# Layer 0 with its side chains at other steps; the state-space stage with taps stacked in three tiles of 96 rows and another order of projections, sums and skips

## The reference, cut to what matters

```python
xz = x @ in_proj_w.T
xi, z = jnp.split(xz_, 2, axis=-1)
xi = silu(causal_dwconv1d(xi))          # 4 taps
x_dbl = xi @ x_proj_w.T                 # dt, B, C
dt = softplus(x_dbl[..., :1] @ dt_proj_w.T + dt_proj_b)
h[t] = exp(dt * A) * h[t-1] + dt * B * u
y = (h * C).sum(-1) + u * D ; y = y * silu(z)
out = (y_forward + y_backward) @ out_proj_w.T
```

## Time and profile before

| | |
|---|---|
| median of 3 runs | 28376.06 us (28369.96 to 28379.99) |
| the profiled execution | 28380.97 us, its span 28379.2 us |
| PE busy | 21447.4 us (76%) |
| DVE busy | 15597.7 us (55%) |
| ACT busy | 14062.1 us (50%) |
| POOL busy | 9313.7 us (33%) |
| granted TensorE clock, mean | 0.907 of full speed |

### The profile page before, as it was taken

How to read it: one execution, slowest core, us unless ns; L and a number is a source line. 1 busy time by engine, 2 the same in 40 slices (tenths; PEclk the granted TensorE clock), 3 DMA queues, 4 the chain that set the end, 5 groups by cost and what they waited for, 6 DMA issues and landing times. The chain is left out here.

```text
span 28379.2 us, 395153 instructions
## 1 busy us (share of the span) xinstructions
PE 21447.4 (76%) x133726; PEld 8244.4 (29%) x134574; DVE 15597.7 (55%) x17851; ACT 14062.1 (50%) x24598; POOL 9313.7 (33%) x7704
## 2 busy tenths in 40 slices
PE   5777777777544777777775999899934888888899
PEld 2222222222211222222221444444401333333344
DVE  7777777777714777777774555555523333333201
ACT  5667666667533555555553666666622222222111
POOL 4666666666403666666664000100000000000000
PEclk9888888888777999999998999999967999999999
DMA  1000000000192000000002010111086010101101
GB/s 56 9 9 9 9 9 9 9 9 9 54 161 73 6 6 6 6 6 6 6 6 69 22 24 22 24 28 24 21 187 157 23 27 20 29 20 28 38 30 47
DMA packets 862945, 933.77 MB, mean 33 GB/s; under 512 B 279812, under 2 KB 754344, under 8 KB 825984
## 3 DMA queue, kind: packets, MB, share of 16 engines
q1 hardware_dynamic: 824904, 819.95, 13.0%
q0 software_dynamic: 17664, 67.11, 0.8%
q10 hardware_dynamic: 19368, 33.14, 0.4%
HBM read 708.43 MB, written 211.63 MB: 32 GB/s over the span
## 5 line engine op out<-in xcount | busy, mean ns | idle before, releaser
L270 DVE TENSOR_TENSOR l_mx<-l_p_v,l_puN 128x2048 f32<-128x2048 f32 x2560 | 5687.2, 2283 | 1797.8 <-PE l_p_s L485 1464.6
L485 PE MATMUL l_p_s<-l_mx,l_w2z 128*32 128x512 f32 x32768 | 4246.7, 657 | 455.5 <-ACT l_mx L397 282.7
L290 POOL TENSOR_TENSOR l_mx<-l_pv,l_puP 128x2048 f32<-128x2048 f32 x1024 | 3706.4, 3640 | 31.9 <-ACT l_puN L363 16.5
L1650 ACT ACTIVATE l1d_ab<-l1d_pt 128x512 f32<-128x512 f32 x4608 | 2739.5, 599 | 1570.7 <-PE l1d_pt L1488 1484.3
L1583 DVE TENSOR_SCALAR l1d_hat<-l1d_ab 128x512 f32<-128x512 f32 x4608 | 2039.0, 443 | 2092.0 <-ACT l1d_ab L1650 1988.0
L1197 POOL TENSOR_TENSOR l1m_hc<-l1m_hs,l1m_cs 128x512 f32<-128x512 f32 x2304 | 2921.8, 1268 | 9.2 <-DVE l1m_hs L1149 9.1
L1884 PE MATMUL l3a_p<-l3a_xn,l3a_w 128*128 128x512 f32 (+1 forms) x6144 | 2678.8, 599 | 274.6 <-ACT l3a_xn L1775 274.6
L1149 DVE TENSOR_TENSOR_SCAN l1m_hs<-l1m_da,l1m_carry,l1m_pu 128x512 f32<-128x512 f32 x2304 | 2824.1, 1267 | 106.1 <-ACT l1m_da L1063 2.2
L397 ACT ACTIVATE l_mx<-l_mx 128x2048 f32<-128x2048 f32 x1024 | 1945.3, 1906 | 1367.8 <-POOL l_mx L290 1367.0
L1990 POOL DMA_DIRECT2D l3b_xt<-x_after x64 | 33.9, 530 | 7646.2 <-DVE l3b_most L2119 5820.6
L416 ACT ACTIVATE l_mx<-l_pv,l_puP 128x128 f32<-128x128 f32 x8192 | 2443.8, 391 | 0.0
(11 more groups left out here) (304 smaller groups left out, 25533.3 us busy)
## 6 DMA issues: line engine op xcount, KB each, us to landing
n_xt<-x_after SPq DMA_DIRECT2D x48, 2048.0 KB
l3a_xb<-x_after SPq DMA_DIRECT2D x352, 256.0 KB, 4.1
l1o_img<-x_after SPq DMA_DIRECT2D x32, 2032.0 KB, 17.5
l_img<-x_after SPq DMA_DIRECT2D x32, 2032.0 KB, 17.5
n_xt<-in_x_dram SPq DMA_DIRECT2D x16, 2048.0 KB
l_xs<-in_x_dram SPq DMA_DIRECT2D x128, 256.0 KB, 3.0
x_after<-l_ot SPq DMA_DIRECT2D x128, 256.0 KB, 2.4
l1o_img<-x_after SPq DMA_DIRECT2D x16, 2048.0 KB, 16.6
```

Of the source, the lines that this page charges most:

```text
L270: v.tensor_tensor(mx[:, r % QB, :, :, :], columns.unsqueeze(1).broadcast_to([P, 4, G, P]), rows.broadcast_to([P, 4, G, P]), ALU.max).then_ ...
L290: g.tensor_tensor(mx[:, r % QB, :, :, :], pv[:, u, :, :].unsqueeze(1).broadcast_to([P, 4, G, P]), rows.broadcast_to([P, 4, G, P]), ALU.add ...
L485: ins = pe.matmul(p_s[R * q:R * (q + 1), 512 * u:512 * (u + 1)], w2z[:, 31 - r:63 - r], mx[:, r % QB, q, :, :].rearrange("p t v -> p (t v) ...
L1650: act.activation(ab[:, n % 3, :], pt[:, 512 * (n % 3):512 * (n % 3 + 1)], ACT.Abs).then_inc(abs_done, 1)
```

## The change

Layer 0: the string of makers is rotated (the same 20 "v", 8 "g" and 4 "a"), and 14 side steps get other step numbers. State-space: the four taps become rows of three tiles of 96 rows (4 x 72 = 288 = 3 x 96), so `sq` holds four shifted copies of a chunk and is filled by six transfers instead of one; x_proj has three matmuls instead of four; z_proj reads the third tile with zero weights for the rows that it does not need. Four memsets that padded the tiles go, with their waits. z_proj of half 0 moves from p = 0 to p = 1, dt_proj of half 0 from p = 4 to p = 3, the sums over pairs 0 to 3 to p = 5, the sum over pairs 5 and 6 to p = 7, the output projection to p = 8; ScalarE follows; the skip and the gates move by one pair or one part, and dt of half 1 moves on GpSimd from p = 6 to p = 7.

```diff
-MAKERS = "vvgvvavgvvgvvavgvvgvvavgvvgvvavg"
+MAKERS = "agvvvgvvagvvvgvvagvvvgvvagvvvgvv"
...
 (gpsimd)
-                    if before is not None and r == 6:
+                    if before is not None and r == 13:
                         weigh_sums(i - 1)
-                    if before is not None and r == 15:
+                    if before is not None and r == 14:
                         finish(i - 1, 1 - u, before)
-                    if r == 19:
+                    if r == 31:
                         modulate(i, u)
...
 (scalar)
-            prepare = {16: normalise, 21: copy_hT, 28: copy_projections, 31: copy_corrections}
+            prepare = {17: normalise, 19: copy_hT, 26: copy_projections, 28: copy_corrections}
...
-                    if before is not None and r == 6:
+                    if before is not None and r == 5:
                         sigmoids(i - 1, 1 - u)
-                    if before is not None and r == 10:
+                    if before is not None and r == 13:
                         copy_aT(i - 1)
-                    if before is not None and r == 14:
+                    if before is not None and r == 16:
                         copy_z(i - 1)
-                    if r == 18:
+                    if r == 22:
                         copy_mT(i)
...
 (tensor)
-                    if before is not None and r == 3:
+                    if before is not None and r == 7:
                         weighted_sums(i - 1, 1 - u)
-                    if before is not None and r == 6:
+                    if before is not None and r == 8:
                         mix(i - 1, 1 - u)
-                    if r == 9:
+                    if r == 16:
                         modulation(i, u)
-                    if following is not None and r == 13:
+                    if following is not None and r == 16:
                         transposes(i + 1, 1 - u)
-                    if following is not None and r == 20:
+                    if following is not None and r == 22:
                         projections(i + 1, 1 - u)
-                    if following is not None and r == 26:
+                    if following is not None and r == 24:
                         pe.wait_ge(mT_ready, i + 1)
                         corrections(i + 1, 1 - u)
...
+TILE_ROWS = 96
+TAP_PARTS = ((0, 0, 0, 72), (0, 72, 0, 24), (1, 0, 24, 48), (1, 48, 0, 48), (2, 0, 48, 24), (2, 24, 0, 72))
...
-                sp.dma_start(sq[0:R, u, :], seq[at(i)].rearrange("i p n -> (i p) n")).then_inc(s_in[u], 16)
+                taps = (0, 1, 1, 2, 2, 3)
+                rows = seq[at(i)].rearrange("i p n -> (i p) n")
+                for tap, (tile, to, first, n) in zip(taps, TAP_PARTS):
+                    sp.dma_start(sq[to:to + n, u, tile, :], rows[first:first + n, tap:tap + LC]).then_inc(s_in[u], 16)
...
-                for tap in range(4):
-                    ins = pe.matmul(pp[:, :], wtap[:, tap, hf, :], sq[:, un, tap:tap + LC], start=tap == 0, stop=tap == 3)
+                for tile in range(3):
+                    ins = pe.matmul(pp[:, :], wtap[:, tile, hf, :], sq[:, un, tile, :], start=tile == 0, stop=tile == 2)
...
 (tensor, chunk)
                     if p == 0 and not last:
                         x_proj(n, un, 0)
-                        z_proj(n, un, 0)
                     if p == 1:
                         reduce_previous(i, u)
+                    if p == 1 and not last:
+                        z_proj(n, un, 0)
                     if p == 2 and not last:
                         x_proj(n, un, 1)
                         z_proj(n, un, 1)
-                    if p == 3:
+                    if p == 5:
                         reduce(i, u, (0, 1))
+                        reduce(i, u, (2, 3))
+                        reduce(i, u, (4,))
+                    if p == 7:
+                        reduce(i, u, (5, 6))
                     if not last:
+                        if p == 3:
+                            dt_proj(n, un, 0)
                         if p == 4:
-                            dt_proj(n, un, 0)
                             dt_proj(n, un, 1)
...
-                    if p == 5:
-                        reduce(i, u, (2, 3))
-                    if p == 6:
-                        reduce(i, u, (4,))
-                    if p == 7:
+                    if p == 8:
                         out_proj(i, use_of(N, 0) if last else use_of(n, OUT))
-                    if p == 8:
-                        reduce(i, u, (5, 6))
...
 (vector)
-                    if p == 1:
+                    if p == 2:
                         skip(i - 1, 1 - u, 1, i * D_IN + (8 + 4))
```

More of the change, by code:

```diff
@@ L748, in state_space @@
         m = Memory(nc, ctx, "l1m")
-        win = m.sb("win", [P, 4, P])
-        crow = m.sb("crow", [R, 4, 2, P])
-        wtap = m.sb("wtap", [P, 4, 2, P])
+        wx = m.sb("wx", [TILE_ROWS, 3, 2, P])
+        wz = m.sb("wz", [TILE_ROWS, 2, P])
+        crow = m.sb("crow", [TILE_ROWS, 3, 2, P])
+        wtap = m.sb("wtap", [TILE_ROWS, 3, 2, P])
         wdt = m.sb("wdt", [P, 2, 2, P])
@@ L760, in state_space @@
         slt = m.sb("slt", [P, RUNS, 32])
-        sq = m.sb("sq", [P, 2, HALO + LC])
+        sq = m.sb("sq", [TILE_ROWS, 2, 3, LC])
         al = m.sb("al", [NB, 2, D_IN + 1])
@@ L790, in state_space @@
         stored = [m.sem("stored0"), m.sem("stored1")]
-        TILES = 4
-        WEIGHTS = 12
+        LOADS = 16 * len(TAP_PARTS)
+        WEIGHTS = 13
         block = ctx.enter_context(nc.Block())
@@ L861, in z_proj @@
                 into_pp(n, (Z0, Z1)[hf])
-                pe.matmul(pp[:, :], win[:, 2 + hf, :], sq[:, un, HALO:], start=True, stop=True).then_inc(pp_full, 1)
+                pe.matmul(pp[:, :], wz[:, hf, :], sq[:, un, 2, :], start=True, stop=True).then_inc(pp_full, 1)
             def both_halves(out, w, n_in):
@@ L949, in _ @@
             reduce_previous(0, 0, (5, 6))
-            pe.wait_ge(s_in[0], 16)
+            pe.wait_ge(s_in[0], LOADS)
             x_proj(0, 0, 0)
@@ L973, in chunk @@
                     if p == 0 and not last:
-                        pe.wait_ge(s_in[un], jn * 16 + 16)
+                        pe.wait_ge(s_in[un], jn * LOADS + LOADS)
                         x_proj(n, un, 0)
-                        z_proj(n, un, 0)
                     if p == 1:
@@ L1087, in chunk @@
                         decays(n, un, p + 2 - PAIRS)
[L1088 to L1097, removed]
-                    if not last:
+                    if not last:
+                        if p == 0:
+                            gate_x(n, un, 0, True)
+                        if p == 1:
+                            gate_z(n, un, 0, True)
+                        if p == 2:
+                            a_of(n, un, jn)
+                            gate_x(n, un, 1, True)
+                            gate_z(n, un, 1, True)
+                        if p == 3:
+                            softplus_parts(n, 0, True)
                         if p == 4:
-                            softplus_parts(n, 0, True)
                             softplus_parts(n, 1, True)
@@ L1106, in chunk @@
                             c_copy(n, un, True)
+                    if p == 8:
+                        out_copy(j, u, use_of(N, 0) if last else use_of(n, OUT))
             over_chunks(act, chunk)
@@ L1112, in _ @@
         def _(dve):
-            for tile in (win, wtap, sq, wo):
-                dve.memset(tile[:], 0.0).then_inc(padded, 1)
             dve.memset(hc[:], 0.0).then_inc(hc_done, 6)
@@ L1124, in _ @@
             dve.wait_ge(w_load, 16 * WEIGHTS)
-            dve.wait_ge(padded, TILES)
-            for tap in range(4):
-                dve.tensor_tensor(wtap[0:R, tap], win[0:R, 0:2, :], crow[:, tap], ALU.mult)
+            dve.tensor_tensor(wtap[:], wx[:], crow[:], ALU.mult)
             for hi in range(2):
@@ L1203, in chunk @@
                         outputs(i, j, u, p, part, last)
-                        if (p, part) == (1, 0):
+                        if (p, part) == (2, 0):
                             gated(i - 1, 1 - u, 1)
-                        if (p, part) == (8, 0):
+                        if (p, part) == (8, 1):
                             g.wait_ge(pp_drained, (use_of(N, 0) if last else use_of(i + 1, OUT)) + 1)
                             gated(i, u, 0)
-                        if not last and part == 1 and p in (5, 6):
-                            steps(i + 1, 1 - u, p - 5)
+                        if not last and part == 1 and p in (5, 7):
+                            steps(i + 1, 1 - u, p // 7)
             over_chunks(g, chunk)
@@ L2182, in program @@
     sequences(nc, offsets, tables[2], a["gn_offset_w"], a["gn_offset_b"], seq, B)
[L2183 removed]
+    state_space(nc, seq, a["w_x"], a["w_z"], a["conv_rows"], a["conv_b"], a["w_dt"], a["dt_rows"], a["dt_b"], a["w_b"], a["w_c"],
                 a["a_log"], a["keeps"], a["d_skip"], a["w_out"], a["sel"], a["sel_t"], mixed, B)
```

(21 more changed lines are left out.)

15 lines of the change are left out of this document (5 added, 10 removed).

## The result

The changed kernel takes 26044.35 us (median of four runs, 25924.9 to 26065.4) against 28375.78 us: a ratio of 0.917, 95% interval 0.9157 to 0.9184, so 8.3% faster. The forecast was 25755 us with a range of 25350 to 26950; the gain is 2331 us where 2621 were forecast. The profiled execution took 26026.6 us, its span 26024.8 us. The shortest of the four, 25924.9 us, had a mean granted clock of 0.913 where the other three had 0.906 or 0.907.

What follows compares the result with a forecast made beforehand. Waits between in-order queues, not a full engine, were taken to bound both stages. From the profiled 28381 us, 1638 for layer 0 and 985 for the state-space stage came off; median 5 us lower: 25755 us, range 25350 to 26950.

Steps and rivals of the forecast that it cites:

- What bounds the stages: Both stages: no engine is full, so waits between queues that run in order bound them and new places of steps matter.
- Layer 0: First stage: a group falls from 58.4 to 45.5 us because its long waits go; gain 1638 us.
- The walk: One round followed step by step with trace durations; in layer 0 ScalarE's loop came to 44.1 us, VectorE's to 44.2.
- the 2.4 at `mix`: Layer 0 before the change: a further VectorE idle stretch of about 2.4 us, called the rest of the 14.0 a group.
- The state-space stage: Second stage: a chunk falls from 48.66 to 40.9 us; gain 985 us.
- p = 2 to 4: State-space stage: intervals between `replicate` starts, together 14.4 us a chunk for 16.4, with the longest, 7.9, at p = 2.
- I keep that: 40.9: State-space stage: clean chunk of 40.0 us, plus the old mean's excess of 0.95 at granted clock 0.97, gives 40.9.
- The tap tiles: State-space stage: six x_proj records instead of eight, 1.7 us of work less a chunk, places mattering more.
- rows of 72: x_proj in the state-space stage: half the rows of an array do not change a column rate that such rows already have.
- The rule against it: TensorE's clock: short pauses between matmul groups can make it swing; the forecast held that by the rows it rises.
- Rival 2: TensorE gets a clock of about 0.8 in both stages, some 50 us a group and 44 a chunk: 26720; chance 0.12.
- Hidden costs: State-space stage: six transfers hidden, else 460 us at most; two more table loads already in the walk; GpSimd's wait covered.

Runs made afterwards that it cites:

- sums_back: The changed kernel with `weighted_sums` and `mix` back behind steps 3 and 6 of layer 0 on TensorE; 26420.61 us, 0.9313 of the kernel before.
- makers_only: The kernel before with the new string of makers in layer 0, side steps at their old numbers; 27421.35 us, ratio 0.9671.
- sides_only: The kernel before with the new numbers of layer 0's side steps, old string of makers; 27747.81 us, ratio 0.9783.
- z_twice: The changed kernel with the z projection of half 0 computed twice into the same bank; 25769.09 us, 0.9085 of the kernel before.
- order_only: The kernel before with the new order of the state-space stage on all engines, four taps and one load as before; 27391.03 us, ratio 0.9659.
- x_four: The changed kernel with the first matmul of each x_proj done twice, three tiles and six loads kept; 25917.59 us, 0.9136 of the kernel before.

## Why the prediction was right, and where its sum was off

- **What bounds the stages**: right. Waits between queues were the reserve, 14 us a group and 15 us a chunk over the floors; the change took 13.4 and 5.1 us of them.
- **Layer 0**: right step by step. The walk closed at 44.2 us; I added 1.3 for table loads and hand-overs, and 0.8 was needed (45.02). Each wait that the walk named came as walked: none at `weighted_sums`, 1.2 us at `mix` (1.4), 2.26 at `normalise` (2.2), none at the change of group. `sums_back` shows the first of these to be cause and not company, and `makers_only` with `sides_only` give 12.2 of the 13.4 us one by one. One sum of the reading before does not close: 4.6, 5.6, 2.9 and 2.4 us are 15.5, not 14.0, so the 2.4 at `mix` is not "the rest". The group that was read is longer (59.9 us from one first VectorE step to the next) than the mean. Two slips of rounding do not matter: 58.4 less 44.2 is 14.2, not 14.1, and 28381 less 1638, 985 and 5 is 25753, not 25755.
- **The state-space stage**: direction right, size off by 336 us (649 for 985). The intervals of the walk against the trace are p = 0: 3.6 and 3.85; p = 1: 5.1 and 4.87; p = 2 to 4: 14.4 and 18.7 (10.09 + 5.31 + 3.34); p = 5: 7.4 and 7.41; p = 6 to 8: 9.5 and 9.39. So one term was wrong, p = 2 to 4, and within it the step "I keep that: 40.9", which carried the old clock of 0.97 into an order that had new pauses. TensorE loses its full clock in each chunk, mostly there; `z_twice` shows the cause by filling one pause. Where the clock holds, the walk holds: in the chunk of `order_only` that starts its p = 2 at 10020.88 us, p = 2 to 4 take 7.81 + 3.50 + 2.98 = 14.3 us for 14.4. That the kernel without the tiles then takes the forecast 40.9 us a chunk (41.00) is in part luck, since the forecast was made for three tiles.
- **The tap tiles**: wrong in sign. I counted 1.7 us of work less a chunk. Measured, 0.5 us in the old order, and a loss of 2.55 us in the new one. With less work between the same pauses the clock fell more often and stayed down longer; `x_four` bears out a part of this and leaves a part open. The premise "rows of 72" was misread: x_proj before works on 128 rows. Six records of 96 rows still took 2.84 us at full clock, as forecast (2.85).
- **The rule against it**: the second failure mode of the clock in the Trainium skill (TensorE: Matmul & The Clock Gate, "A second HAM failure mode: psum-queue depth-cycling") speaks of short pauses that make the clock swing. I set it aside because the old stage had waits of up to 3 us at a clock of 0.97. By that rule, the new trace agrees: 0.87 with pauses of 1.54 and 0.68 us. But `order_only` has 0.97 with the same two, so the pauses alone do not give the clock. It did not hold for layer 0, where the clock rose to 0.97. Rival 2, whose chance was 0.12, thus came near in one stage: a chunk of 43.55 us at 0.87, where it gave 44 us at 0.8. In the other it did not. The total lies 289 us above the forecast mainly because the state-space stage gave 336 us less than forecast and layer 0 only 59 us more.
- **Hidden costs**: right. The six transfers are issued within 2.8 us on an idle queue and nobody waits for them; the two more table loads (eight a chunk) lie where the walk put them; GpSimd waits 1.2 us a chunk for the logarithms, and VectorE's scans wait for nothing (106.4 us idle in the stage, 106.1 before).

## What to carry to other kernels

Where all queues run in order and no engine is full, walk one round with the durations of the trace: which wait ends last at each place, and how much each consumer has to spare. Such a walk gave one stage to 0.5 us in 45, and it said what two of the seventeen step numbers (the diff changes 17, not 14) are worth: up to 3 us a group, where 3.2 were measured. But the walk holds only at the clock that its durations were taken at. Check in it where TensorE pauses twice in short order, and what it has to do in between: taking matmuls away there can cost more than they took, and a moved sum can move the loss. Before keeping two edits together, time each alone; here one of them cost 350 us inside a gain of 2331.

## What had not been expected of the hardware

A useless matmul of 0.86 us a chunk gained 1.9 us a chunk, since TensorE then spent 4.1 us of a chunk at 1.2 GHz instead of 11.2. In three chunks of four of the changed kernel the fall came after pauses of no more than 1.54 us, while the old order went through pauses of 2.14 and 3.00 us at a clock of 0.97 over the stage (between 9400 and 11700 us it spent 3.2 us a chunk at the lower level): the longest pause alone does not tell whether the clock falls. And the loss comes back in a regular rhythm: the changed kernel's chunks repeat as 42.77, 42.73, 44.34 and 44.24 us, those of `x_four` as 41.83 and 43.50 (starts of the output's copy on ScalarE).
